# A graph layer on one core: x transposed inside the loop over groups, sums of edges behind long matmuls, 156 counted groups

## The chip, the cores and the metric

The kernel runs on one core of a Trainium2 chip. The metric is the device time of one execution in microseconds; the median of several runs is compared. TensorE does the matrix products (its weight loads are a row of their own, PEld), VectorE (DVE) the comparisons and additions, ScalarE (ACT) the copies out of PSUM, GpSimd (POOL) issues gathers from memory, SyncE (SP) the plain loads.

## The reference, cut to what matters

```python
# x: 3125 nodes x 128; src, dst: 53125 edges, sorted by dst; edge: 53125 x 128
msg = x[src] + edge
neigh = segment_sum(msg, dst, 3125)
rst = (1.0 + eps[0]) * x + neigh
h = rst @ W1 + b1                       # 3125 x 256
h = relu((h - mean(h, 0)) * rsqrt(var(h, 0) + 1e-5) * gamma + beta)
out = layernorm(x + h @ W2 + b2)
```

## The kernel before

The edges are cut into 208 groups of 256 (128 partitions, 2 edges each). As dst is sorted, the edges of a group end at nodes in a window of at most 20 neighbouring columns of `aggT`, the transposed sum over nodes (128 x 3125). The loop `for w in range(G)` takes one group per step; a step is called a window here, from 0 to 207. On TensorE a window begins with the two **sums of edges** (`edge_sum`, L617): edge rows as weights (float32), a 0/1 matrix of 20 columns as the moving operand, result in PSUM, which VectorE adds to `aggT` at the group's first column (L936).

The part x[src] is done in two ways:

- **gathered groups** (58 of them, every third or fourth window): POOL gathers the rows of x with two indirect DMAs per group, which add onto the edge rows in `egat` (L389, seven slots). SP refills a slot when the window that used it has been summed. Nothing else is to be done for such a group; it is called a G window.
- **counted groups** (150, C windows): TensorE counts how often each of the 3125 nodes is a source of each of the 20 columns, with matmuls of 25, 300 and 400 float16 columns (L632, L635, L638; comparisons on VectorE make their operands, `hits_k`). ScalarE copies the counts to `cnt` (L468). Later `cnt` is multiplied by x, which is held as three bfloat16 parts in `xp`, 25 tiles of nodes, so 75 matmuls for each **block** of columns (`multiply`, L609).

The counted groups come first in order of dst, the gathered ones last, and the windows mix them so that POOL works all the while. `BLOCKS_C` cuts the counted groups into blocks; the 75 multiplies of a block are spread over the windows between its completion and that of the next one. The last block is multiplied after the loop. The blocks before are 114, 362, 450, 452, 422, 302 and 198 columns wide; their multiplies run from window 14, 47, 89, 130, 169 and 197 on and after window 207.

Ahead of the loop TensorE transposes x (25 tiles, L552), and ScalarE scales it into `aggT` (L452), where the sums are added. All seven pieces must be there before the loop starts: `pe.wait_ge(x_scaled, NB)` and the same wait on VectorE. In the first windows VectorE and ScalarE also split x into its parts (`rest` L884, `part_3` L892, L473, L475). After the loop come the products with W1 (L567), the statistics, W2 and the layer norm, which the change leaves alone.

There are branches for inputs that don't fit the windows; they aren't taken in these runs.

Of the kernel before, what the change touches and what calls it, by code (L numbers as in the profile page):

```python
# [23 lines left out]
GROUPS_C = 150  # L24
BLOCKS_C = (10, 24, 30, 30, 28, 20, 8)
# [18 lines left out]
PARTS = 3  # L44


def gnn_layer(nc, x, src, dst, edge, eps, w1, b1, gamma, beta, w2, b2, out):
# [52 lines left out]
    assert CHUNKS * CHUNK * D * ROWS >= D and NG > SLOTS and 4 * (NB - 1) + 1 == NT  # L100
# [10 lines left out]
    with ExitStack() as ctx:  # L111
# [22 lines left out]
        dcol = part(T)  # L134
        rl = part(2 * BANK).rearrange("p (a n) -> p a n", a=2)
        at[0] = 0
# [12 lines left out]
        diff = sb("diff", [P, P])  # L149
# [22 lines left out]
        key = sb("key", [P, T, 2], F16)  # L172
        lo = sb("lo", [P, T, 2], F16)
        carry = sb("carry", [P, GC])
        srci = sb("srci", [P, T], I32)
# [4 lines left out]
        hit_g = sb("hit_g", [P, BATCHES, BATCH * ROWS, WIN])  # L180
# [4 lines left out]
        bst = sb("bst", [P, HH, NB, 6])  # L185
# [7 lines left out]
        lst = sb("lst", [P, NT, 6])  # L193
        lag = sb("lag", [P, NT, 2])
        lsd = sb("lsd", [P, NT])
        lrs = sb("lrs", [P, NT])
        lnb = sb("lnb", [P, NT])
# [52 lines left out]
        gen_rows_made = sem("gen_rows_made")  # L250
        gen_rows_turned = sem("gen_rows_turned")
# [43 lines left out]
        def pieces(b):  # L295
            return 4 * b, min(4 * b + 4, NT)

# [71 lines left out]
        def _(pool):  # L369
            nc.gpsimd.memset(xN[:, NT - 1, :], 0.0).then_inc(x_padded, 1)  # L370
            nc.gpsimd.iota(diff[:, :], [[1, P]], base=0, channel_multiplier=-1,
# [20 lines left out]
            with pool.If(flag != 0):  # L392
                nc.gpsimd.iota(iota_b, [[1, BANK]], base=0, channel_multiplier=0,
                               allow_small_or_imprecise_dtypes=True).then_inc(gen_iota_made, 1)
                with pool.Fori(0, G) as g:
                    pool.wait_ge(gen_messages_made, g * 2)
                    nc.gpsimd.tensor_copy(idx[:, 0:ROWS],
                                          srci[:, bass.ds(g * ROWS, ROWS)]).then_inc(gen_indices_staged, 1)
# [4 lines left out]
            with pool.Else():  # L403
                for n in range(NG):
                    k = n % SLOTS
                    pool.wait_ge(slot_loaded[k], 16 * (n // SLOTS) + 16)
                    for j in range(ROWS):
                        m = (GC + n) * ROWS + j
                        gather(egat[:, k, j * D:(j + 1) * D], srci[:, m:m + 1], ALU.add).then_inc(slot_gathered[k], 16)
# [9 lines left out]
        def _(act):  # L419
# [25 lines left out]
            for a in range(2):  # L445
                last = nc.scalar.activation(lo_v[:, :, :, a], ps[:, 4, 0:T].rearrange("p (k q) -> p q k", q=Q), ACT.Copy)
            last.then_inc(lo_made, 1)

            act.wait_ge(b2_ready, 2)
            for b in range(NB):  # L450
                act.wait_ge(x_turned, b + 1)
                nc.scalar.activation(aggT[:, b * BANK:b * BANK + width(b)], ps[:, b % 2, 0:width(b)], ACT.Copy,  # L452
                                     scale=b2e[:, D:D + 1]).then_inc(x_scaled, 1)

            act.wait_ge(path_known, 1)
            flag = act.value_load(wide[0:1, 0:1], min_val=0, max_val=1)
            with act.If(flag == 0):
# [571 lines left out]
```

## Time and profile before

| | us |
|---|---|
| median of 3 runs | 291.31 (289.94 to 293.26) |
| the profiled execution, its own time | 290.88 |
| its span, first to last instruction | 289.1 |
| TensorE busy | 257.7 |
| POOL busy | 195.6 |
| VectorE busy | 199.1 |
| ScalarE busy | 129.1 |

The span is from the first to the last instruction; the rest of the execution's time lies around it. A busy TensorE is not one at its peak: the granted clock tells at which of two levels, 1.2 and 2.4 GHz (0.5 and 1.0), it ran.

### The profile page before, as it was taken

The numbers are of one execution on the slowest core, as the hardware profiler recorded it, in microseconds if no ns is written. First come the engines' busy times: TensorE is split into PE (matmuls) and PEld (weight loads), VectorE is DVE, ScalarE is ACT, GpSimd is POOL, SyncE is SP. The second block draws the span as 40 slices with busy tenths as digits, with TensorE's granted clock in tenths as the row PEclk, the third lists the DMA queues.
The fourth block names the chain that finished last, engine by engine and source line by source line (L and its number), as shares of the span: only waits on it lengthen the run. The fifth ranks groups of instructions, "written<-read, shape, count | busy, mean of one in ns | idle before, by whom it ended". The sixth has DMA issues, their size and how long they took to land.

```text
span 289.1 us, 6643 instructions
## 1 busy us (share of the span) xinstructions
PE 257.7 (89%) x1995; PEld 218.9 (76%) x1995; DVE 199.1 (69%) x896; ACT 129.1 (45%) x230; POOL 195.6 (68%) x129
## 2 busy tenths in 40 slices
PE   1587799999999999999989798888989999999980
PEld 1465599998988999988868687766868888944870
DVE  3869965556556989788877687676767761178991
ACT  0456643332333555555544344344444423076594
POOL 2078888888886788888888888888888889100000
PEclk9996555555556999999999999999999999999995
DMA  6954566656665888887886777776776641000033
GB/s 174 288 148 92 120 130 145 127 139 134 128 137 112 210 194 201 189 202 165 190 206 133 165 163 164 157 149 153 174 151 145 114 72 17 2 0 0 3 107 114
DMA packets 51308, 39.14 MB, mean 135 GB/s; under 512 B 5323, under 2 KB 50299, under 8 KB 51273
## 3 DMA queue, kind: packets, MB, share of 16 engines
q1 hardware_dynamic: 32877, 30.62, 36.5%
q0 software_dynamic: 16704, 7.61, 22.1%
q10 hardware_dynamic: 1692, 0.48, 0.9%
q8 instruction: 17, 0.28, 0.4%
q14 instruction: 18, 0.15, 0.2%
HBM read 37.10 MB, written 1.60 MB: 134 GB/s over the span
## 4 chain that ended last, share of the span: by engine, by line
PE 55%; DMA 14%; issue 9%; DVE 8%; POOL 8%; ACT 4%; SPq 1%; DVEq 0%; ACTq 0%; POOLq 0%
PE ps L617 19%; PE ps L609 18%; POOL egat L389 8%; PE ps L638 7%; DMA egat<-in_x_dram,srci 6%; PE ps L635 5%; DMA egat<-in_edge_attr_dram 4%; DMA xN<-in_x_dram 4%; PE ps L567 4%; ACT big L504 3%; DVE xp L892 1%; DVE big L983 1%; DVE rows L884 1%; PE ps L632 1%; DVE big L985 1%
## 5 line engine op out<-in xcount | busy, mean ns | idle before, releaser
L389 POOL DMA_INDIRECT egat<-in_x_dram,srci x116 | 186.6, 1608 | 50.3 <-issue 32.5
L468 ACT ACTIVATE big<-ps 128x500 f32 x150 | 91.6, 611 | 127.3 <-PE ps L638 127.0
L609 PE MATMUL ps<-big,xp 128*128 128x114 f16 (+6 forms) x525 | 137.8, 310 | 0.0
L617 PEld LDWEIGHTS ps<-hit_c,ebuf 128*128 128x128 f32 x600 | 112.4, 219 | 10.5 <-DVE aggT L936 3.6
L617 PE MATMUL ps<-hit_c,ebuf 128*128 128x20 f32 x600 | 99.6, 256 | 3.6 <-DVE aggT L936 2.4
L609 PEld LDWEIGHTS ps<-big,xp 128*128 128x128 bf16 x525 | 87.4, 172 | 2.8
L936 DVE TENSOR_TENSOR aggT<-aggT,ps 128x20 f32 x208 | 36.0, 173 | 61.3 <-PE ps L617 55.5
L638 PE MATMUL ps<-hit_k,hit_l 128*128 128x400 f16 x150 | 57.0, 380 | 0.0
L617 PEld LDWEIGHTS ps<-hit_g,egat 128*128 128x128 f32 x232 | 42.7, 221 | 18.0 <-issue 9.4
L863 DVE TENSOR_TENSOR hit_k<-iota_k,key 128x400 f16<-128x400 f16 x150 | 54.0, 360 | 0.0
L617 PE MATMUL ps<-hit_g,egat 128*128 128x20 f32 x232 | 40.0, 262 | 10.0 <-DMA egat<-in_x_dram,srci 8.9
L635 PE MATMUL ps<-hit_k,hit_l 128*128 128x300 f16 x150 | 48.0, 320 | 0.0
L861 DVE TENSOR_TENSOR hit_k<-iota_k,key 128x300 f16<-128x300 f16 x150 | 46.4, 310 | 0.1
L857 DVE TENSOR_TENSOR hit_l<-iota_k,lo 128x256 f16<-128x256 f16 x150 | 42.9, 286 | 5.0 <-PE ps L638 2.8
L632 PE MATMUL ps<-hit_n,hit_l 128*128 128x25 f16 x149 | 29.4, 197 | 0.0
L635 PEld LDWEIGHTS ps<-hit_k,hit_l 128*128 128x128 f16 x150 | 15.9, 106 | 9.4 <-issue 0.5
L632 PEld LDWEIGHTS ps<-hit_n,hit_l 128*128 128x128 f16 x149 | 16.4, 110 | 0.2
L638 PEld LDWEIGHTS ps<-hit_k,hit_l 128*128 128x128 f16 x150 | 15.3, 102 | 0.0
L482 ACT ACTIVATE big<-ps,col 128x512 f32<-128x512 f32 (+1 forms) x14 | 8.6, 633 | 9.6 <-PE ps L567 9.5
L833 DVE TENSOR_TENSOR hit_c<-iota_w,rel 128x160 f32<-128x160 f32 (+1 forms) x38 | 12.0, 315 | 0.0
L695 PE MATMUL ps<-w_sb,big 128*128 128x128 f32 (+1 forms) x100 | 11.6, 276 | 0.0
L695 PEld LDWEIGHTS ps<-w_sb,big 128*128 128x128 f32 (+1 forms) x100 | 11.2, 189 | 0.3 <-issue 0.2
(99 smaller groups left out, 148.4 us busy)
## 6 DMA issues: line engine op xcount, KB each, us to landing
ebuf<-in_edge_attr_dram SPq DMA_DIRECT2D x75, 256.0 KB, 3.2
egat<-in_edge_attr_dram SPq DMA_DIRECT2D x57, 128.0 KB, 2.7
egat<-in_x_dram,srci POOLq DMA_INDIRECT x116, 4.0
out_dram<-big SPq DMA_DIRECT2D x6, 256.0 KB
w_sb<-in_L_gnn_W_dram ACTq DMA_DIRECT2D x2, 128.0 KB, 6.7
rows<-in_dst_dram SPq DMA_DIRECT2D x1, 192.0 KB
rows<-in_src_dram ACTq DMA_DIRECT2D x1, 192.0 KB
egat<-in_edge_attr_dram SPq DMA_DIRECT2D x1, 66.0 KB
```

The lines of the kernel that those rows point to most:

```text
L389: return nc.gpsimd.indirect_dma_start(to, None, x[:, :], bass.IndirectOffsetOnAxis(ap=ix, axis=0), compute_op=op)
L468: nc.scalar.activation(cnt[:, :, bass.ds(lows[m % LOADS], WIN)], ps[:, m % BANKS_C, 0:KEYS].rearrange("p (t n) -> p t n", n=WIN), ACT.Copy ...
L609: last = nc.tensor.matmul(ps[:, ACC + f % 2, 0:SIZES[f]], xp[:, t, n, :], cnt[:, t, STARTS[f]:STARTS[f] + SIZES[f]], start=(u == 0), stop= ...
L617: last = nc.tensor.matmul(ps[:, SUMS + w % BANKS_S, 0:WIN], rows_v[:, j * D:(j + 1) * D], hits_v, start=(j == 0), stop=(j == ROWS - 1))
L632: nc.tensor.matmul(o[:, :, 0], hit_l[:, (m - 1) % RING_K, 1, :], hit_n[:, (m - 1) // CARRY % 2, (m - 1) % CARRY, :], start=True, stop=Fals ...
L635: nc.tensor.matmul(o[:, :, 0:WIN_A], hit_l[:, r, 0, :], hit_k[:, r, 0:KEYS_A].rearrange("p (t n) -> p t n", n=WIN_A), start=(m == 0), stop ...
L638: nc.tensor.matmul(o[:, :, FROM_B:WIN], hit_l[:, r, 1, :], hit_k[:, r, KEYS_A:KEYS_A + KEYS_B].rearrange("p (t n) -> p t n", n=WIN_B), sta ...
L695: last = nc.tensor.matmul(ps[0:r, (b + 4) % 8, k:k + D], hT[:, h, t * P:t * P + r], w2_sb[:, h, :], start=False, stop=(h == HH - 1), skip_ ...
L857: nc.vector.tensor_tensor(hit_l[:, r, :, :].rearrange("p j (n two) -> p j n two", two=2), pairs(iota_k[:, 0:P]).unsqueeze(1).to_broadcast( ...
L861: nc.vector.tensor_tensor(pairs(hit_k[:, r, 0:KEYS_A]), pairs(iota_k[:, 0:KEYS_A]), key[:, 2 * m:2 * m + 1, :].to_broadcast([P, KEYS_A // ...
L863: nc.vector.tensor_tensor(pairs(hit_k[:, r, KEYS_A:KEYS_A + KEYS_B]), pairs(iota_k[:, FROM_B:FROM_B + KEYS_B]), key[:, 2 * m + 1:2 * m + 2 ...
L936: nc.vector.tensor_tensor(to, to, ps[:, SUMS + v % BANKS_S, 0:WIN], ALU.add).then_inc(window_added, 1)
```

## The change

- **x is transposed inside the loop.** `turn_x` puts three tiles into each of the first nine windows, one behind each window's first sum and two behind its second. The order `X_ORDER` takes piece 0 first and then in turn the pieces that gathered and counted groups need. ScalarE scales a piece after each of the first seven copies of counts. VectorE waits before each of the first 28 additions only for the pieces under them. The two banks used are those of the blocks.
- **x is split into parts at half the pace**: a piece every second window (`SPREAD = 2`), and the first block's multiplies wait piece by piece.
- **The order within a window**: the block's multiplies are in two halves. In a C window: first half, sum 0, the 25- and 300-column counts, sum 1, the 400-column count, second half. In a G window: first half, sum 0, second half, sum 1.
- **156 counted groups and 52 gathered** (every fourth window), instead of 150 and 58.
- **Nine blocks** instead of seven: 114, 180, 256, 376, 468, 466, 302, 120 and 110 columns; multiplied from window 14, 30, 52, 86, 127, 168, 195 and 206 on, and after window 207.
- The zeroing of `cnt`'s spare columns moves from the front of VectorE's loop to window 14, the first three key comparisons are made in another order, and several buffers are smaller or share memory.

```diff
-GROUPS_C = 150
-BLOCKS_C = (10, 24, 30, 30, 28, 20, 8)
+GROUPS_C = 156
+BLOCKS_C = (10, 12, 17, 25, 31, 31, 20, 8, 2)
...
+SPREAD = 2
+X_RATE = 3
+LATE = 14
+BATCHES_G = 2
...
+        def columns_of(g):
+
+            return max(0, nominal(g) - MARGIN) // BANK, min(N - 1, nominal(g) + MARGIN + WIN) // BANK
+
+        early_g = columns_of(GC)[0]
+        X_ORDER = [0] + [b for i in range(NB) for b in (early_g + i, 1 + i) if (b < NB if b >= early_g else b == 1 + i)]
+        X_ORDER = list(dict.fromkeys(X_ORDER))
+        X_TILES = [(i, t) for i, b in enumerate(X_ORDER) for t in range(*pieces(b))]
...
+            def scale_x(i):
+
+                b = X_ORDER[i]
+                act.wait_ge(x_turned, i + 1)
+                nc.scalar.activation(aggT[:, b * BANK:b * BANK + width(b)], ps[:, ACC + i % 2, 0:width(b)], ACT.Copy,
+                                     scale=b2e[:, D:D + 1]).then_inc(x_scaled, 1)
...
                     if m < NB:
-                        t0, t1 = pieces(m)
+                        scale_x(m)
+                    if m % SPREAD == SPREAD // 2 - 1 and m // SPREAD < NB:
+                        b = m // SPREAD
+                        t0, t1 = pieces(b)
...
-            pe.wait_ge(x_loaded, 32)
-            for b in range(NB):
-                if b >= 2:
-                    pe.wait_ge(x_scaled, b - 1)
-                t0, t1 = pieces(b)
-                for t in range(t0, t1):
+            def turn_x(n0, n1):
+
+                for n in range(n0, min(n1, NT)):
+                    i, t = X_TILES[n]
+                    t0, t1 = pieces(X_ORDER[i])
                     r = rows_of(t)
                     k = (t - t0) * P
-                    last = nc.tensor.transpose(ps[:, b % 2, k:k + r], xN[0:r, t, :], ident[0:r, 0:r])
-                last.then_inc(x_turned, 1)
+                    if n == 0:
+                        pe.wait_ge(x_loaded, 32)
+                    if t == t0 and i >= 2:
+                        pe.wait_ge(x_scaled, i - 1)
+                    last = nc.tensor.transpose(ps[:, ACC + i % 2, k:k + r], xN[0:r, t, :], ident[0:r, 0:r])
+                    if t == t1 - 1:
+                        last.then_inc(x_turned, 1)
...
-            pe.wait_ge(x_scaled, NB)
...
-                    ua, ub = u0 + (u1 - u0) // 3, u0 + 2 * (u1 - u0) // 3
+                    ua = u0 + (u1 - u0 + 1) // 2
                     multiply(f, u0, ua)
...
                     edge_sum(w, 0, rows_v, hits[:, h, :])
-                    multiply(f, ua, ub)
+                    turn_x(X_RATE * w, X_RATE * w + 1)
+                    if w in C_OF:
+                        counts_a(C_OF[w])
+                    else:
+                        multiply(f, ua, u1)
                     edge_sum(w, 1, rows_v, hits[:, h + 1, :])
-                    multiply(f, ub, u1)
+                    turn_x(X_RATE * w + 1, X_RATE * (w + 1))
                     if w in C_OF:
-                        counts(C_OF[w])
+                        counts_b(C_OF[w])
+                        multiply(f, ua, u1)
...
-                dve.wait_ge(x_scaled, NB)
...
+                        b0, b1 = columns_of(g)
+                        if v < 4 * NB or b0 != b1:
+                            dve.wait_ge(x_scaled, max(X_ORDER.index(b) for b in range(b0, b1 + 1)) + 1)
                         dve.wait_ge(window_summed, v + 1)
...
-                    if w < NB:
-                        rest(w)
-                    if 1 <= w <= NB:
-                        part_3(w - 1)
+                    if w % SPREAD == 1 and w // SPREAD < NB:
+                        rest(w // SPREAD)
+                        part_3(w // SPREAD)
```

How it moves instructions, first on TensorE where the loop begins. Before: the transposes, the branch, and then windows 0 and 1, each with its two sums together.

```order
L552 MATMUL ps<-ident,xN 128x128 x24
L552 MATMUL ps<-ident,xN 128x53
...
L617 MATMUL ps<-hit_c,ebuf 128x20 x2
L635 MATMUL ps<-hit_k,hit_l 128x25x12
L638 MATMUL ps<-hit_k,hit_l 128x25x16
L617 MATMUL ps<-hit_c,ebuf 128x20 x2
L632 MATMUL ps<-hit_n,hit_l 128x25
L635 MATMUL ps<-hit_k,hit_l 128x25x12
L638 MATMUL ps<-hit_k,hit_l 128x25x16
```

After, window 0 and the start of window 1 (L649 are the sums, L578 the transposes, L669 and L675 the counts of 300 and 400 columns):

```order
L649 MATMUL ps<-hit_c,ebuf 128x20
L578 MATMUL ps<-ident,xN 128x128
L669 MATMUL ps<-hit_k,hit_l 128x25x12
L649 MATMUL ps<-hit_c,ebuf 128x20
L578 MATMUL ps<-ident,xN 128x128 x2
L675 MATMUL ps<-hit_k,hit_l 128x25x16
L649 MATMUL ps<-hit_c,ebuf 128x20
L578 MATMUL ps<-ident,xN 128x128
```

The 25 transposes no longer stand ahead of the first sum; they lie between the sums of windows 0 to 8.

Then TensorE in the windows of the first block, before: a C window and a G window, with two multiplies (L609) each.

```order
L617 MATMUL ps<-hit_c,ebuf 128x20
L609 MATMUL ps<-big,xp 128x114
L617 MATMUL ps<-hit_c,ebuf 128x20
L609 MATMUL ps<-big,xp 128x114
L632 MATMUL ps<-hit_n,hit_l 128x25
L635 MATMUL ps<-hit_k,hit_l 128x25x12
L638 MATMUL ps<-hit_k,hit_l 128x25x16
L609 MATMUL ps<-big,xp 128x114
L617 MATMUL ps<-hit_g,egat 128x20
L609 MATMUL ps<-big,xp 128x114
L617 MATMUL ps<-hit_g,egat 128x20
```

After, around window 30, where the second block (180 columns) begins; L641 are the multiplies, L666 the count of 25 columns:

```order
L649 MATMUL ps<-hit_c,ebuf 128x20
L675 MATMUL ps<-hit_k,hit_l 128x25x16
L641 MATMUL ps<-big,xp 128x114 x2
L641 MATMUL ps<-big,xp 128x180 x2
L649 MATMUL ps<-hit_c,ebuf 128x20
L666 MATMUL ps<-hit_n,hit_l 128x25
L669 MATMUL ps<-hit_k,hit_l 128x25x12
L649 MATMUL ps<-hit_c,ebuf 128x20
L675 MATMUL ps<-hit_k,hit_l 128x25x16
L641 MATMUL ps<-big,xp 128x180 x3
L649 MATMUL ps<-hit_g,egat 128x20
L641 MATMUL ps<-big,xp 128x180
```

The sum after a window's 300-column count now stands behind it, where a short multiply stood ahead of it, and there are four or five multiplies in a window for two.

## Rows read from the trace of the kernel before

**Rows 1.** The page: granted clock in 40 slices of the span, and the gathers' group.

```profile
PEclk9996555555556999999999999999999999999995
...
L389 POOL DMA_INDIRECT egat<-in_x_dram,srci x116 | 186.6, 1608 | 50.3 <-issue 32.5
```

**Rows 2.** The waits (us in total, times, longest).

```profile
POOL egat L389 <- DMA egat<-in_edge_attr_dram: 17.9, 10, 12.7
PEld ps L617 <- issue: 11.0, 8, 2.3
PE ps L617 <- DMA egat<-in_x_dram,srci: 8.9, 8, 1.9
```

**Rows 3.** The gathers' line L389 alone: shortest, median and longest, first and last start.

```profile
L389 POOL DMA_INDIRECT egat<-in_x_dram,srci x116: 1543/1546/3006, 15.4 to 238.0; - x116
...
DMA to landing us min/median/max: 3.2/4.0/5.7
```

**Rows 4.** Stretches: length, busy us of PE, PEld, DVE, ACT, POOL, granted clock, DMA share, GB/s.

```profile
20.00:25.00 5.00, 3.06 (x23) 2.26 (x23) 4.05 (x13) 3.42 (x8) 4.09 (x4) 0.82 0.46 86
...
40.00:60.00 20.00, 20.00 (x127) 18.29 (x125) 11.09 (x52) 6.74 (x12) 16.95 (x11) 0.50 0.62 131
60.00:80.00 20.00, 20.00 (x127) 18.30 (x126) 11.76 (x53) 6.76 (x11) 16.65 (x12) 0.50 0.63 139
...
100.00:120.00 20.00, 20.00 (x201) 18.32 (x201) 18.09 (x90) 11.03 (x18) 16.64 (x12) 1.00 0.83 200
...
160.00:180.00 20.00, 17.11 (x155) 14.56 (x155) 14.54 (x69) 7.90 (x13) 16.64 (x12) 1.00 0.73 162
```

**Rows 5.** Timeline where the loop begins: start, us, engine, line, operation.

```profile
14.16 6.01 PE L552 MATMUL ps<-ident,xN 128*128 128x128 f32 x25 [2.16 <-DMA xN<-in_x_dram]
...
15.68 0.81 DVE L903 MEMSET big<- 128x900 uint32 x1 [1.84 <-issue]
...
21.42 0.59 PE L617 MATMUL ps<-hit_c,ebuf 128*128 128x20 f32 x4 [1.24 <-ACT aggT L452]
```

**Rows 6.** Timeline, PE, multiplies of 114 columns: first sums of windows 17 to 20.

```profile
45.62 0.57 PE L617 MATMUL ps<-hit_g,egat 128*128 128x20 f32 x2
...
46.54 0.57 PE L617 MATMUL ps<-hit_c,ebuf 128*128 128x20 f32 x2
...
48.08 0.46 PE L617 MATMUL ps<-hit_c,ebuf 128*128 128x20 f32 x2
...
49.51 0.46 PE L617 MATMUL ps<-hit_c,ebuf 128*128 128x20 f32 x2
```

**Rows 7.** Timeline, PE, where the 362-column block begins: its first multiply, first sums of windows 48 and 49.

```profile
86.40 0.47 PE L609 MATMUL ps<-big,xp 128*128 128x362 f16 x1
...
87.28 0.46 PE L617 MATMUL ps<-hit_c,ebuf 128*128 128x20 f32 x2
...
89.00 0.46 PE L617 MATMUL ps<-hit_c,ebuf 128*128 128x20 f32 x2
```

**Rows 8.** Timeline, PE, full clock, 362-column block: first sums of windows 59 to 61.

```profile
98.09 0.29 PE L617 MATMUL ps<-hit_c,ebuf 128*128 128x20 f32 x2
...
99.00 0.29 PE L617 MATMUL ps<-hit_g,egat 128*128 128x20 f32 x2
...
99.58 0.52 PE L617 MATMUL ps<-hit_c,ebuf 128*128 128x20 f32 x4
```

**Rows 9.** Timeline, PE: first sums of windows 179, 197 and 207.

```profile
213.10 0.37 PE L617 MATMUL ps<-hit_g,egat 128*128 128x20 f32 x2 [0.79 <-DMA egat<-in_x_dram,srci]
...
231.65 0.29 PE L617 MATMUL ps<-hit_g,egat 128*128 128x20 f32 x2
...
245.37 0.29 PE L617 MATMUL ps<-hit_g,egat 128*128 128x20 f32 x2
```

**Rows 10.** Timeline, PE: part of the last block (198 columns), and the first product with W1.

```profile
249.78 3.06 PE L609 MATMUL ps<-big,xp 128*128 128x198 f16 x34
252.68 10.90 PE L567 MATMUL ps<-aggT,w_sb 128*128 128x512 f32 x28
```

More of the change, by code:

```diff
@@ L134, in gnn_layer @@
         dcol = part(T)
+        src_all = part(T).bitcast(I32)
         rl = part(2 * BANK).rearrange("p (a n) -> p a n", a=2)
+        bst = part(HH * NB * 6).rearrange("p (h b s) -> p h b s", h=HH, b=NB)
+        lst = part(NT * 6).rearrange("p (t s) -> p t s", s=6)
+        lag = part(NT * 2).rearrange("p (t s) -> p t s", s=2)
+        lsd, lrs, lnb = (part(NT) for _ in range(3))
         at[0] = 0
@@ L171, in gnn_layer @@
         rel = sb("rel", [P, T])
-        key = sb("key", [P, T, 2], F16)
-        lo = sb("lo", [P, T, 2], F16)
+        key = sb("key", [P, GC * ROWS, 2], F16)
+        lo = sb("lo", [P, GC * ROWS, 2], F16)
         carry = sb("carry", [P, GC])
-        srci = sb("srci", [P, T], I32)
+        srci = sb("srci", [P, NG * ROWS], I32)
         idx = sb("idx", [P, ROWS], I32)
@@ L620, in edge_sum, with counted, counts_a @@
                         last.then_inc(window_summed, 1)
-                def counts(m):
-                    r = m % RING_K
-                    o = ps[:, m % BANKS_C, 0:KEYS].rearrange("p (t n) -> p t n", n=WIN)
+                def counted(m):
+                    return ps[:, m % BANKS_C, 0:KEYS].rearrange("p (t n) -> p t n", n=WIN)
+                def counts_a(m):
                     pe.wait_ge(key_hits_made, m + 1)
@@ L792, in _ @@
             for a in range(2):
-                last = nc.vector.tensor_copy(key_d[:, :, :, a], banked(3))
+                last = nc.vector.tensor_copy(key_d[:, :, :, a], banked(3)[:, 0:QC, :])
             last.then_inc(slots_made, 1)
@@ L899, in add_block @@
                     nc.vector.tensor_tensor(v, v, ps[:, ACC + f % 2, 0:SIZES[f]], ALU.add).then_inc(block_added, 1)
-                dve.wait_ge(carry_turned, 1)
-                dve.wait_ge(lo_turned, 1)
-                nc.vector.memset(cnt[:, :, CNT - SPARE:CNT], 0.0).then_inc(spare_zeroed, 1)
                 dve.wait_ge(constants_made, 7)
+                dve.wait_ge(lo_made, 1)
+                hits_k(0)
                 hits_c(0)
+                hits_k(1)
+                hits_n(0)
+                hits_k(2)
                 hits_g(0)
-                dve.wait_ge(lo_made, 1)
-                for m in range(AHEAD):
-                    hits_k(m)
-                hits_n(0)
                 dve.wait_ge(x_loaded, 32)
-                dve.wait_ge(x_scaled, NB)
                 dve.wait_ge(src_rows_made, 1)
```

87 lines of the change are left out of this document (47 added, 40 removed).

## Prediction

> **What bounds the kernel now.** I read three views. First the page's row of the granted clock [rows 1] and the table of stretches [rows 4]: TensorE is at full clock (1.0) up to some 23 us, at half (0.5, 1.2 GHz) until about 91 us, and full for the rest of the loop. Second the gathers: POOL is busy 16.64 to 16.95 us in every 20 us [rows 4], whatever the others do. It issues 116 gathers from 15.4 to 238.0 us [rows 3], one each 1.608 us plus the 0.3 us of issue that the waits on "issue" come to (32.5 us over 106 times) [rows 1]: 1.908 us, and 115 x 1.908 = 219.4 of the 222.6 us. The 3 us left are waits for refilled slots (17.9 less the first, 12.7, and partly the same issue) [rows 2]. Third the waits of TensorE: 8.9 us for gathers and 11.0 us of weight loads on "issue", the same stalls [rows 2], seen as PE 17.11 busy of 20 [rows 4]. So there are three stretches. At first TensorE is late, since half clock costs it its lead. Once it has caught up with the gathers it waits for them, the last time at window 179, 213.10 us [rows 9]. From there its own work sets the time: 18.55 us to window 197, 13.72 us for the ten windows to 207, and 7.3 us to the first product with W1 at 252.68 [rows 9, 10]. VectorE follows; ScalarE is never near.
>
> **The change part by part.** All of it lies ahead of that first product; the 36.4 us of span behind it (289.1 - 252.68) and the 1.8 us around the span (290.88 - 289.1) stay.
>
> **Fewer gathers.** 12 of 116 go: 12 x 1.908 = 22.9 us less on POOL. POOL's first gather stays at 15.4 us (the same indices, the same wait for the branch), so the last starts at 15.4 + 103 x 1.908 = 211.9. What follows on POOL, the addition of b2, stays long before its use. As gathered groups now come every fourth window, the gathers set a pace of 2 x 1.908 / 4 = 0.954 us a window. Window 167, the 42nd G window, needs gathers 83 and 84: 15.4 + 83 x 1.908 + 4.0 to land [rows 3] = 177.8 us, and window 168 can't start before about 178.6.
>
> **TensorE at full clock.** The C window of the 362-column block took 0.91 us, the G window 0.58 [rows 8]; each holds two multiplies. A multiply costs its columns at 2.4 GHz plus 0.006 us (34 of 198 columns in 3.06 us is 0.088 each after the tail of the last, 0.0825 of it the columns [rows 10]), so 0.157, and what is left is 0.59 for a C and 0.265 for a G window with both sums behind something long. Check: windows 197 to 206 are 7 C and 3 G windows with 68 multiplies of 302 columns: 4.13 + 0.80 + 68 x 0.132 = 13.9, measured 13.72 [rows 9]. For 179 to 197 the same sum gives 17.8 and the trace 18.55, so I add 1 us for such losses. With three C windows to one G, a window without multiplies is 0.509 us. The blocks after, 75 multiplies each: windows 14 to 29, 12.1 us; 30 to 51, 17.3; 52 to 85, 25.8; 86 to 126, 33.1; 127 to 167, 36.0; 168 to 194, 28.7; 195 to 205, 15.5; 206 and 207, 5.2; the last block 75 x 0.052 = 3.9. Up to window 167 this is 0.76 to 0.88 us a window, below the gathers' 0.954; from 168 on it is 1.06 and more, above. So TensorE should wait for the gathers up to 168 and set the end from there.
>
> **The early start.** The transposes (6.01 us) and the wait for ScalarE go from the front of the loop [rows 5]. TensorE then waits for VectorE, which begins at 15.7 [rows 5] and needs about 1 us for the first comparisons: window 0 at about 17 instead of 21.42. Before, window 14 came at about 41.8 (window 17 at 45.62 less two C and a G window, 3.8 [rows 6]), 20.4 us after window 0, with VectorE the slowest; it has the same key comparisons and splits of x in them. The 25 transposes now lie in its shadow, ScalarE's seven copies too (it was busy 3.42 of 5 us there [rows 4]). If that cover fails, the transposes cost their 5 us or so again. I take window 14 at 37 us. The wait of VectorE for a scaled piece holds up its own later comparisons, but a piece is turned within three windows of its need; nothing to 1 us.
>
> **Long matmuls ahead of the sums.** At half clock the weight loads are the bound where multiplies are short: a C window took 1.43 to 1.54 us and a G window 0.92 [rows 6]; the 362-column C window took 1.72 [rows 7]. After, a C window of the 114-column block has 534 multiplied columns for that row's 724: 1.72 - 190/1200 = 1.56; of the 180-column block 1.63; of the 256-column block 1.59. With the G windows (0.92 to 1.2) that is 1.45, 1.51 and 1.44 us a window. These are estimates from rows 6 and 7. At full clock the order saves only where one sum stood right behind the other, under 0.1 us in some 40 windows; it is hidden by the gathers' pace, so I count nothing.
>
> **The rest.** Six more counted groups, 92 more columns and two more blocks are in the sum. VectorE was busy 18.09 of 20 us at 0.83 us a window [rows 4, 8]; at 0.954 us and 1.04 times the comparisons it is at 16.4 of 20, no bound. The memset in window 14 (0.81 us, [rows 5]) is work moved.
>
> **When the clock comes back** is the one thing that the sum needs and no row shows. It fell after the idle stretch at the start of the loop (3.06 us busy of 5 [rows 4]), stayed at half through all windows with about two 114-column multiplies, and was back within 5 us of the first 362-column one [rows 4, 7]. The new windows lie between: as full of columns as rows 7 but for some 110 to 190 columns in a C window, and far fuller than rows 6. I take full clock from window 30 at the latest: 37 + 16 x 1.45 = 60.2; then 17.3 + 25.8 + 33.1 + 36.0 brings TensorE to window 168 at 172.4, still 6.2 us ahead of the gathers' 178.6. So it makes no difference if the clock comes back earlier, or up to 9 windows later (0.72 us each).
>
> **The sum.** 178.6 + 28.7 + 15.5 + 5.2 + 3.9 + 1.0 = 232.9 us at the first product with W1, against 252.68: 19.8 us less. 290.88 - 19.8 = 271.1; the median of the runs shown is 0.4 us above the profiled one, so 271.5.
>
> **The Trainium skill against rows.** TensorE counts as busy for all of 40 to 80 us and the clock is 0.50 [rows 4]. The Trainium skill, TensorE: Matmul & The Clock Gate, section "What's actually happening", says that activity releases the throttle and idleness brings it back. With "busy" as the profile marks it the trace disagrees; by that rule the clock would be full from window 14 and the sum the same, since the gathers set it. Likewise POOL's 16.64 us in a stretch with VectorE at 18.09 and 16.65 with VectorE at 11.76 [rows 4]: a denser VectorE doesn't slow gathers. The Trainium skill, SBUF — State Buffer, section "Who interferes with whom", lets a two-input VectorE instruction contend with GpSimd's reads; the trace shows no such price, and the sum has none.
>
> **The rivals.**
> - **The clock comes back only with the third block (256 columns), window 52.** For: its C window differs least from rows 7 in what stands ahead of each sum. Against: the first two blocks are hardly less full. Window 52 at 60.2 + 22 x 1.51 = 93.4, window 168 at 188.3, 9.7 us behind the gathers: 281.
> - **The clock stays at half until the 376-column block, window 86**, the first at least as wide as the one with which it came back before. Window 86 at 93.4 + 34 x 1.44 = 142.4, window 168 at 211.5, 32.9 us late: 304, slower than before. The point from which this turns the sign: full clock not before about window 67, when the 6.2 us in hand and the 19.8 us of gain (the sum above) are used up. In its favour is that no row shows full clock regained with a narrower multiply.
> - **Gathers bind beyond window 168**, because refills come late or VectorE's first windows drag: TensorE's end is then later by up to 5 us: 276. This stands inside my range.
> - **The gain is lost** because several chains near each other stall one another (gathers 0.954, TensorE 0.88, VectorE 0.8 us a window): 0.1 us in each of 200 windows would eat it: 291. The stretch before in which TensorE waited for gathers kept POOL's pace [rows 4], against it.
>
> **Chances.** Forecast (clock back by about window 39; 267 to 277) 0.69; third block 0.13; fourth block 0.09; gain lost 0.04; better than 267 0.05, since the 1 us of losses and the landing time of 4.0 may be high. The range 267 to 285 holds the forecast and the third block's case. Within 1% is about what a measurement of this kernel can tell from no change: faster 0.87, same 0.04, slower 0.09.
>
> **What would show it.** Window 0 at about 17 us; granted clock at 1.0 from some point between windows 14 and 39 (40 to 70 us); POOL's last gather near 212; TensorE's waits for gathers between about 70 and 178 us and none later; the first product with W1 near 233. The prediction is wrong if the half clock lasts beyond 75 us or POOL waits for slots by more than 5 us.

## The result, and the profile after

| | before | after |
|---|---|---|
| median of the runs, us | 290.62 (289.55 to 293.26, 4 runs) | 281.84 (278.38 to 288.98, 4 runs) |
| profiled execution, us | 290.88 | 278.38 |
| its span, us | 289.1 | 276.6 |
| first product with W1, us | 252.68 | 240.16 |

The ratio is 0.9594 with an interval of 0.9469 to 0.9719: faster. Forecast were 271.5 us (267 to 285). The profiled execution is the shortest of the four (278.38, 280.04, 283.63, 288.98); against its forecast of 271.1 it is 7.3 us late, and all of that lies ahead of the first product with W1 (240.16 for 232.9), since the 36.4 us behind it are unchanged. By the medians the change gained 8.8 us where 19.8 were forecast. Where ratios stand below, runs of more than 1.5% above a kernel's fastest are left out of them; medians are over all runs.

The page, where it answers to [rows 1], the gathers' group:

```profile
PEclk9999999999999999999999999999999999999997
...
L402 POOL DMA_INDIRECT egat<-in_x_dram,srci x104 | 171.4, 1648 | 44.5 <-issue 30.2
...
L900 DVE TENSOR_TENSOR hit_l<-iota_k,lo 128x256 f16<-128x256 f16 x156 | 50.9, 326 | 1.7 <-issue 1.6
```

The row of the granted clock misleads here: this trace has no record of the clock ahead of 71.8 us and shows the gap as full. The durations tell. TensorE's timeline around 71.8 us (start, us, engine, line, operation), counts of 400 columns (L675) and sums (L649):

```profile
69.81 0.50 PE L675 MATMUL ps<-hit_k,hit_l 128*128 128x400 f16 x1
...
71.16 0.46 PE L649 MATMUL ps<-hit_c,ebuf 128*128 128x20 f32 x2
...
72.07 0.33 PE L649 MATMUL ps<-hit_g,egat 128*128 128x20 f32 x2
...
73.11 0.33 PE L675 MATMUL ps<-hit_k,hit_l 128*128 128x400 f16 x1
```

A 400-column count takes 0.50 us up to there and 0.33 behind, a pair of sums 0.46 and then 0.33 or 0.29: half clock up to window 35, which begins at 72.07, and full clock from it on.

The waits and the gathers' line, for [rows 2] and [rows 3] (us in total, times, longest; then shortest, median and longest, first and last start):

```profile
POOL egat L402 <- DMA egat<-in_edge_attr_dram: 13.9, 5, 12.7
...
PEld ps L649 <- DVE aggT L979: 7.9, 6, 2.8
```

```profile
L402 POOL DMA_INDIRECT egat<-in_x_dram,srci x104: 1546/1570/4469, 15.4 to 217.0; - x104
...
  PE ps L649: 1.6, 2
```

TensorE waits 1.6 us for gathers instead of 8.9, and now for additions on VectorE (L979). One gather took 4.469 us. The last starts at 217.0, 21 us earlier than before, 5 later than forecast.

Stretches as in [rows 4]:

```profile
40.00:60.00 20.00, 20.00 (x143) 18.18 (x142) 12.00 (x54) 7.09 (x15) 16.95 (x11) 1.00 0.59 122
...
100.00:120.00 20.00, 19.89 (x210) 17.41 (x209) 18.48 (x93) 11.66 (x19) 16.95 (x11) 1.00 0.86 199
160.00:180.00 20.00, 19.45 (x174) 15.72 (x172) 15.93 (x78) 9.67 (x18) 16.65 (x12) 1.00 0.80 177
```

From 160 to 180 us TensorE is busy 19.45 of 20 us, for 17.11 before: it hardly waits there, though the runs below with an earlier clock show the gathers close behind. The start of the loop, for [rows 5]: VectorE, and POOL at its second gather, which took 4.47 us (the held gather from here on):

```profile
15.26 0.29 DVE L900 TENSOR_TENSOR hit_l<-iota_k,lo 128x256 f16<-128x256 f16 x1 [1.61 <-issue]
15.37 1.74 POOL L402 DMA_INDIRECT egat<-in_x_dram,srci  x1 [12.73 <-DMA egat<-in_edge_attr_dram]
...
16.34 0.61 PE L649 MATMUL ps<-hit_c,ebuf 128*128 128x20 f32 x2 [4.10 <-DVE hit_c L876]
...
17.41 4.47 POOL L402 DMA_INDIRECT egat<-in_x_dram,srci  x1 [0.30 <-issue]
...
20.49 0.69 DVE L935 TENSOR_TENSOR xp<-rows 128x512 bf16<-128x512 f32 x1
```

The first sum starts at 16.34 us, 5.1 earlier than before. And the end of the gathers, windows 198 to 202, all engines but ScalarE:

```profile
216.96 1.55 POOL L402 DMA_INDIRECT egat<-in_x_dram,srci  x1 [0.30 <-issue]
...
217.95 7.55 POOL L429 TENSOR_TENSOR xN<-xN,b2e 128x3200 f32<-128x3200 f32 x1
...
218.84 0.18 DVE L979 TENSOR_TENSOR aggT<-aggT,ps 128x20 f32 x1 [1.32 <-PE ps L649]
218.94 6.72 DVE L900 TENSOR_TENSOR hit_l<-iota_k,lo 128x256 f16<-128x256 f16 x1
...
222.16 0.29 PE L649 MATMUL ps<-hit_c,ebuf 128*128 128x20 f32 x2
...
226.08 0.16 DVE L979 TENSOR_TENSOR aggT<-aggT,ps 128x20 f32 x1
...
226.30 0.40 PE L649 MATMUL ps<-hit_c,ebuf 128*128 128x20 f32 x2 [2.49 <-DVE aggT L979]
```

POOL adds b2 to x right behind its last gather, for 7.55 us. A comparison that takes 0.28 us elsewhere is issued 1 us later and ends 0.16 us after POOL's addition: 6.72 us. The additions behind it on VectorE are late, and TensorE, which ran ahead through the free banks, stands still ahead of window 202: the sums of window 201 began at 222.16 and those of 202 at 226.30, where a window there takes 1.5 us. Before, the same addition of 7.56 us began at 238.95, when the last comparison was done (the last one of this kind began at 236.6); beside it VectorE only ran additions out of PSUM, 0.18 us each and unheld.

Window starts in the two profiles, against the forecast (us):

| first sum of window | 0 | 14 | 30 | 52 | 86 | 127 | 168 | 195 | 206 | W1 |
|---|---|---|---|---|---|---|---|---|---|---|
| TensorE's own sum, forecast | 17 | 37 | 60.2 | 77.5 | 103.3 | 136.4 | 172.4, 178.6 with the gathers | 207.3 | 222.8 | 232.9 |
| after | 16.34 | 39.4 | 64.4 | 86.0 | 112.3 | 146.4 | 184.9 | 214.0 | 232.5 | 240.16 |

### The profile page after: what moved, and what is told of

The parts are those of the page before. It is cut to its first block, busy times and chain, and to the rows that moved or that the text cites. A ratio compares the mean times of both kernels' runs of the same rounds, so it can differ in the third digit from the quotient of the medians.

```text
span 276.6 us, 7007 instructions
## 1 busy us (share of the span) xinstructions
PE 251.1 (91%) x2163; PEld 212.4 (77%) x2163; DVE 207.5 (75%) x916; ACT 132.1 (48%) x236; POOL 180.4 (65%) x117
## 3 DMA queue, kind: packets, MB, share of 16 engines
q0 software_dynamic: 14976, 6.82, 20.5%
## 4 chain that ended last, share of the span: by engine, by line
PE 69%; DMA 8%; issue 6%; DVE 6%; ACT 4%; POOL 3%; SPq 2%; DVEq 0%; ACTq 0%; POOLq 0%
PE ps L641 24%; PE ps L649 21%; PE ps L675 9%; PE ps L669 7%; DMA egat<-in_edge_attr_dram 4%; DMA egat<-in_x_dram,srci 4%; PE ps L595 4%; POOL egat L402 3%; ACT big L527 3%; PE ps L578 2%; PE ps L666 1%; SPq L321 1%; DVE big L1029 1%; DVE big L1031 1%; DVE hit_l L900 1%
## 5 line engine op out<-in xcount | busy, mean ns | idle before, releaser
L402 POOL DMA_INDIRECT egat<-in_x_dram,srci x104 | 171.4, 1648 | 44.5 <-issue 30.2
L488 ACT ACTIVATE big<-ps 128x500 f32 x156 | 95.2, 610 | 115.3 <-PE ps L675 86.0
L649 PEld LDWEIGHTS ps<-hit_c,ebuf 128*128 128x128 f32 x624 | 111.4, 212 | 14.3 <-DVE hit_c L876 4.2
L641 PE MATMUL ps<-big,xp 128*128 128x114 f16 (+8 forms) x675 | 118.9, 287 | 0.0
L649 PE MATMUL ps<-hit_c,ebuf 128*128 128x20 f32 x624 | 102.8, 244 | 6.7 <-DVE hit_c L876 4.1
L641 PEld LDWEIGHTS ps<-big,xp 128*128 128x128 bf16 x675 | 66.0, 114 | 15.5 <-issue 3.3
L979 DVE TENSOR_TENSOR aggT<-aggT,ps 128x20 f32 x208 | 35.8, 172 | 46.3 <-PE ps L649 30.4
L675 PE MATMUL ps<-hit_k,hit_l 128*128 128x400 f16 x156 | 56.2, 360 | 0.0
L900 DVE TENSOR_TENSOR hit_l<-iota_k,lo 128x256 f16<-128x256 f16 x156 | 50.9, 326 | 1.7 <-issue 1.6
L669 PE MATMUL ps<-hit_k,hit_l 128*128 128x300 f16 x156 | 48.7, 312 | 0.0
L649 PEld LDWEIGHTS ps<-hit_g,egat 128*128 128x128 f32 x208 | 36.1, 211 | 7.7 <-DVE aggT L979 5.1
L649 PE MATMUL ps<-hit_g,egat 128*128 128x20 f32 x208 | 34.2, 249 | 2.9 <-DMA egat<-in_x_dram,srci 1.6
L675 PEld LDWEIGHTS ps<-hit_k,hit_l 128*128 128x128 f16 x156 | 30.4, 195 | 0.1
L666 PEld LDWEIGHTS ps<-hit_n,hit_l 128*128 128x128 f16 x155 | 30.3, 195 | 0.0
L666 PE MATMUL ps<-hit_n,hit_l 128*128 128x25 f16 x155 | 29.3, 189 | 0.0
L669 PEld LDWEIGHTS ps<-hit_k,hit_l 128*128 128x128 f16 x156 | 15.7, 100 | 0.4
L876 DVE TENSOR_TENSOR hit_c<-iota_w,rel 128x160 f32<-128x160 f32 x39 | 12.4, 318 | 0.0
```

The source lines that it names most:

```text
L402: return nc.gpsimd.indirect_dma_start(to, None, x[:, :], bass.IndirectOffsetOnAxis(ap=ix, axis=0), compute_op=op)
L488: nc.scalar.activation(cnt[:, :, bass.ds(lows[m % LOADS], WIN)], ps[:, m % BANKS_C, 0:KEYS].rearrange("p (t n) -> p t n", n=WIN), ACT.Copy ...
L641: last = nc.tensor.matmul(ps[:, ACC + f % 2, 0:SIZES[f]], xp[:, t, n, :], cnt[:, t, STARTS[f]:STARTS[f] + SIZES[f]], start=(u == 0), stop= ...
L649: last = nc.tensor.matmul(ps[:, SUMS + w % BANKS_S, 0:WIN], rows_v[:, j * D:(j + 1) * D], hits_v, start=(j == 0), stop=(j == ROWS - 1))
L666: nc.tensor.matmul(counted(m)[:, :, 0], hit_l[:, (m - 1) % RING_K, 1, :], hit_n[:, (m - 1) // CARRY % 2, (m - 1) % CARRY, :], start=True, ...
L669: nc.tensor.matmul(counted(m)[:, :, 0:WIN_A], hit_l[:, m % RING_K, 0, :], hit_k[:, m % RING_K, 0:KEYS_A].rearrange("p (t n) -> p t n", n=W ...
```

## The experiments

Each was timed in five rounds against the kernel before (medians there 289.96 to 290.47 us).

**The changed kernel again.**

> The changed kernel once more, unedited, as the base of the other runs. Expected 278 to 284 us, the spread coming from where the granted clock comes back to full (window 35 in the trace shown; some windows earlier or later in others).

Measured: 281.45 us (278.11 to 289.46, 6 runs), ratio 0.9604 (0.9554 to 0.9654). The profiled run (279.69) shows the same things: clock back at 72.5 us, a comparison of 6.11 us at 220.9, a second gather of 5.1 us. Two of its six runs and one of the four above took 288 to 289 us. The record of those runs gives their mean granted clock, in which a stretch without a record counts as full: 0.864 for 289.46 us and for 288.98 us. An estimate from mean and span is at least 78 us at half clock; a run of 276.09 us of the next kernel, with a mean of 0.905, comes to at least 52. So in these two long runs the clock came back later. The third (288.35, mean 0.969) doesn't tell.

**The addition of b2 after the last comparison.**

```diff
                 pool.wait_ge(x_first_made, NB)
+                pool.wait_ge(key_hits_made, GC)
```

> One wait more: POOL adds b2 to xN only after the last key comparison. Theory (POOL's addition holds up VectorE's comparisons, one of which took 6.72 us from 218.9 us on): no comparison of hit_l over 1 us, TensorE's 4.14 us window at 222 us back to 1.5, and 2.5 to 3.5 us less than the unedited kernel. Rival (the long comparison only mirrors slack that TensorE fills later): within 1 us of it.

Measured: 277.5 us (276.09 to 279.23, 6 runs), ratio 0.9557 (0.9519 to 0.9596). POOL now waits, and the comparisons stay short:

```profile
222.71 0.31 DVE L905 TENSOR_TENSOR hit_k<-iota_k,key 128x300 f16<-128x300 f16 x1
222.94 0.36 DVE L907 TENSOR_TENSOR hit_k<-iota_k,key 128x400 f16<-128x400 f16 x1
...
223.72 6.97 POOL L430 TENSOR_TENSOR xN<-xN,b2e 128x3200 f32<-128x3200 f32 x1 [4.20 <-DVE hit_k L907]
223.88 0.18 DVE L980 TENSOR_TENSOR aggT<-aggT,ps 128x20 f32 x1 [0.58 <-PE ps L650]
```

From window 195 to 206 it takes 15.8 us (215.0 to 230.8) where the changed kernel took 18.6 and 18.0, so the held comparison cost 2.1 to 2.8 us. The whole times say less: the ratios 0.9557 and 0.9604 have overlapping intervals, and the 4 us between the medians hold the long runs too. This is shown: one wait added as the only edit, the long comparison gone, the windows back at their price. The Trainium skill, SBUF — State Buffer, section "Who interferes with whom", states that a VectorE instruction with two SBUF inputs contends with a GpSimd instruction that reads SBUF, that issue order decides which of them blocks, and that one with at most one SBUF input, outside the two-port modes, doesn't contend. These traces agree in all three: the comparison issued 1 us behind the addition of 7.55 us ended with it after 6.72 us, and additions out of PSUM took 0.18 us. All kernels below keep the edit and are compared with this one.

**The window's old order:** multiplies in thirds, all counts behind the second sum.

```diff
-                    ua = u0 + (u1 - u0 + 1) // 2
+                    ua, ub = u0 + (u1 - u0) // 3, u0 + 2 * (u1 - u0) // 3
...
-                    if w in C_OF:
-                        counts_a(C_OF[w])
-                    else:
-                        multiply(f, ua, u1)
+                    multiply(f, ua, ub)
...
+                    multiply(f, ub, u1)
                     if w in C_OF:
+                        counts_a(C_OF[w])
                         counts_b(C_OF[w])
-                        multiply(f, ua, u1)
```

> Late addition, and the order within a window as before (multiplies in thirds around the sums, all counts at the end). If long matmuls ahead of the sums matter only as I forecast (nothing at full clock, under 0.1 us a window at half), the time is 0 to 2 us above the run with the late addition. Rival: the order is what lets the clock come back, then it stays at half until window 52 or later and the time is 6 to 20 us above it.

Measured: 287.09 us (278.16 to 293.41, 8 runs). Three runs are at 278.2 to 279.5 and five at 287.1 to 293.4; the ratio of the short ones is 0.9599 (0.9554 to 0.9644), which is not clear of noise against 0.9557 (0.9519 to 0.9596). The profiled run is a long one (287.1): clock back at 92.7 us, just before window 47, for 72.4; window 52 at 97.2 for 86.6. The stretches show what follows:

```profile
60.00:80.00 20.00, 20.00 (x126) 17.43 (x127) 10.11 (x45) 6.15 (x10) 14.58 (x10) 1.00 0.55 116
80.00:100.00 20.00, 20.00 (x159) 17.69 (x160) 12.54 (x58) 7.24 (x12) 10.09 (x7) 1.00 0.51 117
```

TensorE frees the slots so late that POOL is busy 10.09 us of 20 instead of 16.77 (the record of the clock begins late here too). At full clock the order is worth nothing: from window 52 to 86 it takes 26.2 us with either. What sets the long runs apart is a late return of the clock: the profile shows it for one, and the mean granted clocks of two others (0.853 in the run of 293.41 us, 0.867 in that of 287.09) come to at least 86 and 76 us at half clock, by the same estimate. The other two (0.994, 0.993) don't tell. The changed kernel has such runs too. They are more frequent with the old order, five of eight against three of ten and none of six with the edit above, which suggests that the order moves the clock's return; so few runs don't show it.

**The old cut of the blocks** (114, 362, ... columns in seven blocks; 156 counted groups kept).

```diff
-BLOCKS_C = (10, 12, 17, 25, 31, 31, 20, 8, 2)
+BLOCKS_C = (10, 24, 30, 30, 28, 24, 10)
```

> Late addition, 156 counted groups, but the blocks as wide as before (114, 362, 450, 452, 422 columns and two smaller ones). Theory: in windows 14 to 46 only about two multiplies of 114 columns stand in a window, the clock stays at half until window 48 to 51, near 85 to 90 us, and the time is 3 to 8 us above the run with the late addition. Rival: the clock comes back as soon, since the sums stand behind the counts, and with 150 multiplies fewer the time is 0 to 3 us below it.

Measured: 279.51 us (277.01 to 279.76, 6 runs), ratio 0.9589 (0.954 to 0.9637): 2.0 us longer by the medians, less than expected, and the intervals overlap. The clock comes back at 89.1 us, a few windows after the 362-column block has begun, as in the kernel before. It costs little here, since these windows hold few multiplies: window 30 comes at 61.5 for 65.0 us, window 52 at 90.6 for 86.6, and W1 at 241.5 for 238.4.

**150 counted groups and 116 gathers again.**

```diff
-GROUPS_C = 156
-BLOCKS_C = (10, 12, 17, 25, 31, 31, 20, 8, 2)
+GROUPS_C = 150
+BLOCKS_C = (10, 12, 17, 25, 31, 31, 16, 6, 2)
```

> Late addition, all else as changed, but 150 counted and 58 gathered groups. Theory (twelve gathers fewer are what makes room): the last of 116 gathers starts at 15.4 + 115 x 1.96 = 241 us, TensorE waits for gathers from about window 100 on, and the time is 286 to 292, no gain over before. Rival (TensorE's own work sets the time and six counted groups more cost it): 272 to 276.

Measured: 292.75 us (291.23 to 295.4, 12 runs), ratio 1.0095 (1.0066 to 1.0124), all other parts of the change kept. The waits:

```profile
PE ps L650 <- DMA egat<-in_x_dram,srci: 16.8, 15, 2.1
```

and the gathers' line:

```profile
L402 POOL DMA_INDIRECT egat<-in_x_dram,srci x116: 1545/1580/5077, 15.0 to 239.5; - x116
```

TensorE gets the clock back at 77.5 us, for some 91 before the change, and hands it all back in waits for gathers. The 12 gathers are worth 292.75 - 277.5 = 15.3 us: the whole gain. The rest of the change without them loses 2.3 us. The other way round, 12 gathers fewer on the kernel before and nothing else, was not run, so whether they alone are enough is open.

**A longer stretch of columns at half clock:** one more matmul of 380 float16 columns of constants between the sums, in windows 13 to 27.

```diff
+                    if FILL[0] <= w < FILL[1]:
+                        fill(w)
```

> On top of the late addition, windows 13 to 27 get one more matmul each, 380 columns of constants whose result nobody reads, between the two sums. Theory (what is left of the missing gain is the half clock up to window 35): the clock comes back in the first 10 us after window 13, window 52 comes 6 to 9 us earlier than the 86.0 us of the trace, and the time falls by another 3 to 5 us, where gathers then bind at window 168 near 181 us; the spread between runs shrinks. Rival (gathers bind, or VectorE, whatever the clock): within 1 us of the run without the matmuls, or 2 us slower by their own cost.

Measured: 275.04 us (274.38 to 276.13, 6 runs), ratio 0.9465 (0.9434 to 0.9495); clock back at 49.5 us. The added matmul starts its PSUM bank anew, so one of the two sums of those 15 windows is left out. With start=False they are whole:

> The run with the extra matmuls once more, now adding onto their columns instead of starting them anew, so that the sums beside them stay whole. Expected the same within 1 us as with them before, 275 us: full clock by about window 20, gathers binding up to window 168. The rival, that the lost sums mattered to the time, would show as a difference of over 2 us.

Measured: 274.74 us (274.14 to 275.12, 5 runs), ratio 0.9449 (0.9405 to 0.9493). The page's clock row and TensorE's timeline (L658 is the added matmul, L682 the 400-column count, 0.33 us at 48.16 for 0.50 at 46.27):

```profile
PEclk9999999999999999799999999999999999999995
```

```profile
47.44 0.49 PE L658 MATMUL ps<-iota_k 128*128 128x380 f16 x1
...
48.16 0.33 PE L682 MATMUL ps<-hit_k,hit_l 128*128 128x400 f16 x1
...
48.78 0.32 PE L658 MATMUL ps<-iota_k 128*128 128x380 f16 x1
```

Clock back at 48.0 us instead of 72.4, window 52 at 77.2 for 86.6, and the runs lie within 1 us of each other. But only 2.8 us of the 9.4 reach the end, since TensorE now waits for gathers, 8.5 us for 3.8:

```profile
PE ps L651 <- DMA egat<-in_x_dram,srci: 8.5, 7, 1.6
```

Work that computes nothing made the kernel faster: more columns among the same sums bring the clock back. That is shown for this added matmul in these windows.

The 7 in the clock row is a second stretch at half clock, from 112.9 to 116.3 us. In the 10 us ahead of it TensorE had been busy 8.36 us, with a wait of 1.58 us for a gather at window 91. Windows 93 and 94 took 1.36 and 1.75 us, for 0.92 and 0.91 in the profile of the pause below, which has no such stretch. Five more profiles show such stretches: that of 150 counted groups (two, at 152.6 and 200.4 us), that of the first added matmul, and three of the kernels below (the transposes ahead, twice, and the old front order). Ahead of all seven TensorE was busy 7.0 to 8.5 of 10 us. But the kernel before was busy 7.49 us from 180 to 190 and kept full clock, so what decides it is open.

**The transposes ahead of the loop again** (`turn_x(0, NT)` and the seven scalings before it), first without the added matmul, then with it.

```diff
+                turn_x(0, NT)
                 for w in range(G):
...
-                    turn_x(X_RATE * w, X_RATE * w + 1)
...
-                    turn_x(X_RATE * w + 1, X_RATE * (w + 1))
```

> Late addition, and all 25 transposes and seven scalings ahead of the loop as before; the rest as changed. Theory (TensorE, not the gathers, is late up to window 168 by 1 to 2 us over them): window 0 near 21.4 us for 16.7, window 14 and window 168 2 to 5 us later, the time 2 to 4 us above the run with the late addition. Rival (the gathers hide the start): within 1 us. Second rival: with nothing between the sums of windows 0 to 8, VectorE paces them anyway, window 14 comes at 40 to 42 us and only 1 to 2 us are lost.

> The version with the extra matmul (e6_fill_kept), but with all 25 transposes and the seven scalings ahead of the loop, as in e7_turn_first. There the late start (window 0 at 20.5 us) had been made good by window 14, and the whole differed from the version without it by less than the spread of the runs, of which the changing return of the clock was a part. Here the clock comes back early in all runs, so the two can be told apart. If the transposes in the loop gain nothing: window 14 at 37 to 40, the whole 274 to 275.5. If they gain what was forecast for the start (4 us or more at window 0): the whole 277 to 279.

Measured: 277.89 us (275.77 to 282.85, 6 runs), ratio 0.9521 (0.9467 to 0.9574) against 277.5 and 0.9557; with the added matmul 274.39 us (273.28 to 276.09, 6 runs), ratio 0.943 (0.939 to 0.947) against 274.74 and 0.9449. No difference either time. The windows say why: the first starts at 20.5 and 20.7 us instead of 16.7 and 16.3, but window 14 at 37.4 and 37.9 instead of 39.9 and 39.5. In the first windows VectorE sets the pace, with its comparisons and splits of x, and transposes and scalings that finish ahead spare it waits. The early start is given back before window 9 (30.9 for 34.2 us).

**The second gather.** In each profile of the changed kernels so far it took 4.5 to 5.1 us, for 1.66 before. Three kernels with the added matmul as base (274.74 us). First a wait for POOL in VectorE's front, and then, without it, the old order of the first comparisons:

```diff
+                dve.wait_ge(gather_released, 3)
                 hits_k(2)
```

> The version with the extra matmul (e6_fill_kept) with one wait more: VectorE waits, before its third set of key comparisons (17.15 us), until POOL has issued its second gather. In each run of the changed kernel this gather took 4.5 to 5.1 us and ended as VectorE had its first idle time, for 1.66 us before the change. Theory one, an unbroken run of VectorE holds the gather: it takes 1.7 us now, VectorE goes on at 19.4, the last gather starts 2 to 3 us earlier (214 to 215.5 for 217.3), window 14 comes up to 1.5 us later (41), and as TensorE waits for gathers up to window 168 the whole is 1 to 3 us shorter than 274.7: 272 to 273.7. Theory two, the length of the gather has another cause (the first addition onto fresh rows, or the loads of SP beside it): still 4.5 us or so, the last gather at 217 or later, the whole 274.7 to 276.

> The version with the extra matmul (e6_fill_kept) with VectorE's first comparisons in the order of the kernel before (both 0/1 matrices of sums, three sets of key comparisons, then the 25-column one) and no wait added; VectorE stays without a break for longer. Theory one, an unbroken run of VectorE alone holds the second gather: 4.5 us or more, the whole 274.7 to 276 (window 0 up to 0.3 us earlier). Rival, what counts is which comparisons lie beside the gather's issue: it takes 1.7 us as in the kernel before, last gather 214 to 215.5, the whole 272 to 273.7.

Measured: 274.89 us (273.45 to 275.81, 6 runs) and 274.82 us (273.74 to 276.24, 6 runs). The first tests nothing: the semaphore that POOL raises ahead of each gather was up while the second, begun at 17.52, still ran (to 22.24), and VectorE went on at 17.54 without a gap. In the second the order is the old one and the gather takes 4.87 us: the order is not it. Then a wait that holds:

```diff
+                dve.wait_ge(x_scaled, 1)
                 hits_k(2)
```

> The wait tried before (e8_pause) was met at once and made no pause: VectorE went on at 17.54 us. Here VectorE waits before its third set of key comparisons for the first scaled piece of x, which ScalarE finishes at about 19.8 us, so it is idle from 17.15 to about 19.8. Theory one, an unbroken run of VectorE holds POOL's second gather (4.5 us for 1.66): the gather ends within about 1 us of VectorE's idle start (about 18.5 to 19.2), the last gather starts 2 to 3 us earlier than 217.3, window 14 up to 2.5 us later than 39.5, the whole 272 to 275. Theory two, another cause: the gather still takes 4 us or more, last gather 217 or later, the whole 275 to 277.

Measured: 272.55 us (271.03 to 273.46, 6 runs), ratio 0.9366 (0.9321 to 0.9412), the shortest of all; against 0.9449 (0.9405 to 0.9493) the intervals just touch. VectorE's pause, then POOL's first gathers:

```profile
17.32 0.36 DVE L926 TENSOR_TENSOR hit_n<-iota_c,carry 128x200 f16<-128x200 f32 x1
20.30 0.29 DVE L909 TENSOR_TENSOR hit_l<-iota_k,lo 128x256 f16<-128x256 f16 x1 [2.63 <-ACT aggT L469]
```

```profile
15.59 1.69 POOL L403 DMA_INDIRECT egat<-in_x_dram,srci  x1 [12.97 <-DMA egat<-in_edge_attr_dram]
17.59 1.55 POOL L403 DMA_INDIRECT egat<-in_x_dram,srci  x1 [0.30 <-issue]
19.45 1.54 POOL L403 DMA_INDIRECT egat<-in_x_dram,srci  x1 [0.30 <-issue]
```

With VectorE idle the second gather takes 1.55 us, the mean is 1613 ns for 1655, the last starts at 214.1 for 217.3, and TensorE's waits for gathers fall from 8.5 to 2.7 us. Window 14 comes 1.6 us later and the clock 7.8 us later (55.8), and still W1 is at 234.6 for 236.5. So VectorE's work beside this gather holds it: that much is shown. In all twelve profiles with a held gather it ends 0.7 us after VectorE's first idle moment (21.18 and 21.88 us in the profile of the change). Which of VectorE's instructions hold it is open. "Any run without a gap" is too simple: the kernel before ran VectorE without a gap from 15.68 to 19.28 us beside a gather of 1.66 at 17.36, and its longest (3.01 us, at 32.5) ended in the midst of such a run.

## Why the prediction was right, and what was off in it

The sign, the range and the main cause held; the point was 10.3 us too low against the median, 7.3 against the profiled run. The other 3 come from the longer runs; a late return of the clock accounts for one of the four (288.98 us), the run of 283.63 doesn't tell. The 7.3 us are 6.3 at window 168, 0.4 up to window 195 and 3.1 up to 206, less 1.5 for the last windows and the last block and 1.0 entered for losses. There is luck in the range: it reached to 285 for the case of the clock back with the third block, which the profile doesn't show, and other errors used it up. By its own sign the prediction fails for the run of 288.98 us: its 78 us of half clock, for 52 in a short run, can hardly have ended before 75 us.

- **The 12 gathers** carry the gain, as worked out: without them there is none (292.75 us). Their own pace was underrated by 5.1 us at the last one. Of this 2.9 us is the one held gather, removed in the last experiment, 1.4 us the other gathers (1.622 us each for 1.608) and 0.8 us the idle time between them, of which waits for slots are 0.3 us. The step that failed is "a denser VectorE doesn't slow gathers": the means of 20 us stretches can't show what one instruction does to another. Here TensorE was late by itself, so it cost little at first; once the clock came early the gathers were the bound.
- **TensorE reaches window 168 first, the gathers at 178.6 set it**: wrong. TensorE's own sum was 172.4 and it came at 184.9, waiting only 1.6 us for gathers in all. But the gathers' 178.6 was too early as well: gather 84 started at 179.3 us for 173.8, and with the clock back at 48.0 us window 168 still came at 184.0, 0.9 us earlier than here and 1.9 earlier than in the kernel without the added matmul. So TensorE's lateness decides only 1 to 2 of the 6.3 us there, and the gathers' pace the rest. TensorE's own 12.5 us are: window 14 at 39.4 for 37 (+2.4); windows 14 to 29 in 25.0 us for 23.2 (+1.8), as estimates from rows of other widths; the clock back at window 35 and not 30, with the rest of the block at 0.82 us a window for 0.79 (+4.3 to window 52); 26.3 for 25.8, 34.1 for 33.1 and 38.5 for 36.0 us behind (+4.0), where the prices of a window held (0.79 us with one 468-column multiply, 0.99 with two, 0.67 in a G window, as forecast) and small waits for VectorE's additions and gathers were left out: from window 127 on four windows took 1.11 to 1.88 us where the others with two multiplies took 0.99. The 1.5 us from window 52 to 127 have hardly a wait beside them and stay open. The 1.0 us for losses had been entered only after window 168.
- **Full clock by window 30, with tolerance to 39**: right as a bound in the three profiles of this order with 156 counted groups and the transposes in the loop (71.8 to 72.5 us, window 35), and not in the two long runs whose mean clock tells. But "it makes no difference" was wrong, for the 6.2 us in hand didn't exist. Bringing it to 48 us gained 2.8 us.
- **"Long matmuls ahead of the sums: count nothing"**: right at full clock (26.2 us with either order), and within noise for the short runs. The profiled run of the old order had its clock back 20 us later, but it was a long one, and such runs occur with both orders. Whether the order makes them more frequent is open, and the sum had no term for it.
- **Early start**: window 0 at 16.34 for 17 was right, the 4 us gained by window 14 (37 instead of 41.8) were not: 39.4, and 37.4 when the transposes stand first again. "A piece is turned within three windows of its need; nothing to 1 us" was the failing step: it was VectorE's time that counted there.
- **The addition of b2 "stays long before its use"**: true of its use, and the wrong question. It came 21 us earlier, out of the quiet end into VectorE's comparisons, and cost 2.1 to 2.8 us. "The trace shows no such price" held only because nothing of that kind had overlapped in it: windows 195 to 205 took 18.6 us for 15.5. The last block and windows 206, 207 took 7.6 us for 9.1.
- **Rivals.** The clock's return with the third block (281 us) had the clock back at 93.4 us, near the 92.7 of the old order's profiled run (there before window 47, and 287.1 us in all). The changed kernel's profiles don't show it, though its median is near that number. A half clock to the fourth block was not seen. Gathers binding beyond window 168: in no profile of a changed kernel does TensorE wait for a gather behind window 164, but gathers late by 5 us at 168, which this rival comes to, are what the runs with the early clock show. The lost gain (291) was the fate of the 116 gathers, through waits for them.

## What to carry to other kernels

When a change shortens one queue, look at what stands behind it on that queue and what it will run beside at its new time: an operation that was free at the quiet end can block another engine in the busy part. Give TensorE's clock a term of its own that goes by the matmuls which stand among the short ones, and expect it to vary between runs; then check whether an earlier clock has a bound behind it that takes the gain. Parts that look additive weren't: the start gained nothing, and the clock 2.8 us of 9.4.

## What the runs showed of the hardware

- A float16 comparison with both inputs in SBUF stood for 6.1 to 6.7 us beside a POOL addition of 7.55 us; additions with one input in PSUM took 0.18 us beside the same.
- The issue of POOL's second gather took 4.5 to 5.1 us in the twelve profiles of changed kernels in which VectorE ran on beside it, and ended 0.7 us after VectorE's first idle moment; it took 1.55 us where VectorE paused. The kernel before is the exception: 1.66 us beside a busy VectorE.
- TensorE, marked busy for all of 40 to 70 us, stayed at half clock, and 15 more matmuls of 380 columns brought full clock 24 us earlier. The Trainium skill, TensorE: Matmul & The Clock Gate, section "What's actually happening", ties the clock to activity; with "busy" as the profile marks it that is not enough here.
- One program took 278 to 289 us. In its profiled runs the clock came back at 71.8 and 72.5 us; two of its long runs, with a mean granted clock of 0.864, had at least 78 us at half clock. With the added matmuls the runs took 274.1 to 275.1 us.
- In six profiles the granted clock fell from full to half for 3.4 us within the loop, seven times in all; TensorE had been busy 7.0 to 8.5 of the 10 us ahead. The kernel before kept full clock through 10 us with 7.49 busy.
